# Layer 0: the recurrence's steps on VectorE and GpSimd regrouped, the global context moved into the couplings, the last output projection in two halves

## The reference, cut to what matters

```python
# attention: x + attn(demodulated x), 16 heads of 64
x = x + L0_attn(L0_cond(x, cond), W_qkv, W_out)
# gated recurrence over the 128 tokens, elementwise in the features
f = exp(-(W_f x + b_f));  i = exp(-(W_i x + b_i));  h = W_h x + b_h
#   (the kernel works with F = 1 + f, I = 1 + i, S = F + I + 1e-8 F I,
#    normalised gates I/S and F/S, and three scans along the tokens)
s = recurrence(initial = cond, gates, h)
# feed-forward: three cycles of couplings between features and their "twist"
g  = sigmoid(gc3(gelu(gc2(gelu(gc1(mean over tokens of s))))))   # global context
for cycle in range(3):
    c = base * sigmoid(cn4(gelu(cn3(gelu(cn2(gelu(cn1(s)))))))) + ... g
    s, twisted = s + c * twisted, twisted - c * s
x = x + s
```

## Time and profile before

| | |
|---|---|
| median of 3 runs | 1133.64 us |
| the profiled execution's own time | 1132.62 us |
| its span in the trace | 1131.3 us |
| PE busy | 1015.0 us, 90% of the span |
| DVE busy | 886.0 us, 78% |
| ACT busy | 770.5 us, 68% |
| POOL busy | 458.3 us, 41% |
| mean granted TensorE clock | 0.973 |
| attention of layer 0 with chunks 0 to 6 | start to about 482 us |
| couplings | about 487 to 575 us |

### The profile page before, as it was taken

How to read it: one execution, slowest core, us unless ns; L and a number is a source line. 1 busy time by engine, 2 the same in 40 slices (tenths; PEclk the granted TensorE clock), 3 DMA queues, 4 the chain that set the end, 5 groups by cost and what they waited for, 6 DMA issues and landing times.

```text
span 1131.3 us, 25531 instructions
## 1 busy us (share of the span) xinstructions
PE 1015.0 (90%) x8759; PEld 796.1 (70%) x8759; DVE 886.0 (78%) x3789; ACT 770.5 (68%) x2089; POOL 458.3 (41%) x531
## 2 busy tenths in 40 slices
PE   6999999999999999699889999997888888888677
PEld 5897878788878787533269888885766666665456
DVE  5676869686969686679988888886788888877796
ACT  5876667666766666468768778873677777776442
POOL 2434434343535353408700000006678877784001
PEclk9999999999999999899999999997999999999897
DMA  8000000000000000000000000000000000000002
GB/s 368 1 2 2 2 2 2 1 1 2 2 1 2 2 1 2 1 1 0 1 1 1 1 1 1 10 10 16 16 20 12 21 21 21 20 2 1 1 1 75
DMA packets 8577, 18.32 MB, mean 16 GB/s; under 512 B 1280, under 2 KB 5504, under 8 KB 8064
## 3 DMA queue, kind: packets, MB, share of 16 engines
q1 hardware_dynamic: 8448, 16.69, 4.3%
HBM read 10.39 MB, written 2.10 MB: 11 GB/s over the span
## 4 chain that ended last, share of the span: by engine, by line
PE 55%; DVE 20%; POOL 12%; ACT 8%; issue 5%; DMA 0%; DVEq 0%; ACTq 0%; SPq 0%; POOLq 0%
PE PB L407 5%; PE PB L241 5%; PE PB L242 5%; PE PB L243 5%; POOL AR_s L1525 5%; PE PB L391 4%; PE PB L336 4%; PE PB L374 4%; ACT W L355 3%; PE PB L1059 3%; PE PB L1060 3%; PE PB L1061 2%; DVE W L346 2%; PE PB L425 2%; PE PB L1537 2%
## 5 line engine op out<-in xcount | busy, mean ns | idle before, releaser
L355 ACT ACTIVATE W<-W,small 128x128 f32<-128x128 f32 x512 | 198.6, 390 | 141.8 <-DVE small L346 88.9
L366 POOL TENSOR_TENSOR W<-W,small 128x512 f32<-128x512 f32 x128 | 133.5, 1043 | 269.1 <-DVE small L360 269.1
L241 PE MATMUL PB<-RR_s 128*128 128x256 f32 (+3 forms) x544 | 176.8, 325 | 6.2 <-DVE AR_s L398 2.7
L242 PE MATMUL PB<-RR_s 128*128 128x256 f32 (+3 forms) x544 | 167.2, 307 | 0.0
L243 PE MATMUL PB<-RR_s 128*128 128x256 f32 (+3 forms) x544 | 167.2, 307 | 0.0
L1525 POOL TENSOR_TENSOR AR_s<-AR_s,small 128x512 f32<-128x512 f32 x128 | 129.6, 1040 | 34.9 <-DVE small L1518 34.9
L1033 ACT ACTIVATE AR_s<-PB,W 128x512 f32<-128x512 f32 (+2 forms) x160 | 100.5, 629 | 33.2 <-PE PB L243 28.6
L1047 DVE TENSOR_TENSOR RR_s<-AR_s,RR_s 128x512 fp32r<-128x512 f32 (+2 forms) x160 | 98.9, 622 | 29.7 <-ACT RR_s L1038 26.1
L241 PEld LDWEIGHTS PB<-RR_s 128*128 128x128 f32 x544 | 103.7, 191 | 17.2 <-issue 4.7
L346 DVE CUSTOM_DVE_ANT_0 W<-PB,W 128x128 f32<-128x128 f32 x512 | 113.1, 285 | 2.2
L1518 DVE CUSTOM_DVE_ANT_0 AR_s<-PB,W 128x128 f32<-128x128 f32 x512 | 111.5, 286 | 3.2 <-PE PB L1509 3.0
(11 more groups left out here) (356 smaller groups left out, 2376.5 us busy)
## 6 DMA issues: line engine op xcount, KB each, us to landing
W<-in_w SPq DMA_DIRECT2D x1, 5841.0 KB, 25.0
XF<-in_xT SPq DMA_DIRECT2D x4, 512.0 KB, 9.0
AR_s<-AR_s SPq DMA_DIRECT2D x32, 64.0 KB, 2.1
out<-XT SPq DMA_DIRECT2D x8, 256.0 KB, 2.4
W<-in_w SPq DMA_DIRECT2D x1, 1088.0 KB, 5.1
W<-in_w SPq DMA_DIRECT2D x1, 1024.0 KB, 7.9
QS<-AR_s SPq DMA_DIRECT2D x12, 64.0 KB, 2.1
KR<-AR_s SPq DMA_DIRECT2D x12, 64.0 KB, 2.1
```

What stands on the lines that cost most here:

```text
L241: nc.tensor.matmul(out, lh, rh, start=True, stop=False)
L242: nc.tensor.matmul(out, ll, rh, start=False, stop=False)
L355: e = nc.scalar.activation(SS[r][:, hl], SS[r][:, hl], ACTF.Exp, bias=mx[r][:, h:h + 1], scale=-1.0, accum_out=rc[r][:, h:h + 1])
L366: nc.gpsimd.tensor_tensor(s3, s3, over(rc[r], 2, [128, 4, 128]), ALU.mult).then_inc(s_nrm, 1)
```

## The change

Three edits, all in layer 0.

1. The steps of chunks 0 to 6 are numbered anew. GpSimd's two additions come at step 3 (turn V+1 in place of V+2), and the four reciprocals at steps 4 to 7 (two each in turns V+2 and V+3). GpSimd's two gates come at step 7 (V+3 in place of V+4), VectorE's addition of 1e-8 and GpSimd's h*F at step 8 (V+4 in place of V+5), and the backward scan at step 10 (the same turn V+5, now the only work of the recurrence there on VectorE). What follows stays. For chunk 7 the order on VectorE is the same as it was.
2. The global context of batch elements 0 to 23 leaves turns 64 and 65 of the attention and goes into turns 1 to 3 of the couplings, on banks of `plan3`.
3. The last output projection, `y` number 31, is done in two halves: the first pair of matmuls waits only for the copy of turn 62 and stands at the end of turn 65, the other pair in turn 66. The other projections wait for their two copies one after the other.

```diff
--- before.py
+++ after.py
@@ -221,8 +221,6 @@
                 c, i = divmod(s - 22, 16)
                 if 0 <= c < 7 and i < 3:
                     passes("fih"[i], c, *((s_fe, c + 1), (s_ie, c + 1), (s_gd, c * NGD + HC))[i])
-                if U < s < U + 4:
-                    passes("ctx", s - U - 1, s_cxa, s - U)
             if 0 <= v - 2 < NV:
                 passes("o", v - 2, s_ot, v - 1)
         for i in range(3):
@@ -397,15 +395,16 @@
             dve.wait_ge(s_pv, v + 1)
             nc.vector.tensor_copy(cs(OT[v // 2 % 2], v % 2), bank("o", v)[:, :]).then_inc(s_ot, 1)
 
-        def pe_y(j):
+        def pe_y(j, parts=range(4)):
 
             pe.wait_ge(s_wv, 16)
             pe_drained("y", j)
-            pe.wait_ge(s_ot, 2 * j + 2)
-            for p in range(4):
+            for p in parts:
                 o = (4 * (j % 2) + p) * 128
+                pe.wait_ge(s_ot, 2 * j + p // 2 + 1)
                 mm = nc.tensor.matmul(bank("y", j)[:, 0:256], w("wout", 128, o, o + 128), cs(OT[j % 2], p, 256), start=p == 0, stop=p == 3)
-            mm.then_inc(s_ym, 1)
+            if 3 in parts:
+                mm.then_inc(s_ym, 1)
 
         def dve_y(j):
             c = j // 2
@@ -448,26 +447,26 @@
                 nc.vector.tensor_scalar(IG, IG, 1e22, 1.0, ALU.min, ALU.add).then_inc(s_gd, 1)
                 dve.wait_ge(s_gd, o + GB)
                 nc.vector.scalar_tensor_tensor(SM, FG, 1e-8, IG, ALU.mult, ALU.mult).then_inc(s_gd, 1)
-            if i == 4 and c == CH - 1:
+            if i == 3 and c == CH - 1:
                 dve.wait_ge(s_gd, o + GSUM)
                 nc.vector.tensor_tensor(SM, SM, FG, ALU.add).then_inc(s_gl, 1)
                 dve.wait_ge(s_gl, p + PF)
                 nc.vector.tensor_tensor(SM, SM, IG, ALU.add).then_inc(s_gl, 1)
-            if 5 <= i < 9:
-                bl = bls[i - 5]
+            if 4 <= i < 8:
+                bl = bls[i - 4]
                 dve.wait_ge(s_gl, p + PI)
                 nc.vector.reciprocal(SM[:, bl], SM[:, bl]).then_inc(s_gd, 1)
-            if i == 9 and c == CH - 1:
+            if i == 7 and c == CH - 1:
                 dve.wait_ge(s_gd, o + GR)
                 nc.vector.tensor_tensor(IG, IG, SM, ALU.mult).then_inc(s_gl, 1)
                 nc.vector.tensor_tensor(FG, FG, SM, ALU.mult).then_inc(s_gl, 1)
-            if i == 10:
+            if i == 8:
                 dve.wait_ge(s_gl, p + PIN)
                 nc.vector.tensor_scalar(IG, IG, 1e-8, None, ALU.add).then_inc(s_gd, 1)
                 if c == CH - 1:
                     dve.wait_ge(s_gl, p + PFN)
                     nc.vector.tensor_tensor(SM, cs(HF, c), FG, ALU.mult).then_inc(s_gl, 1)
-            if i == 11:
+            if i == 10:
                 dve.wait_ge(s_const, 4)
                 dve.wait_ge(s_gd, o + GTF)
                 dve.wait_ge(s_gl, p + PNI)
@@ -498,16 +497,16 @@
         def pool_gated(c, i):
 
             o, p = c * NGD, c * NGL
-            if i == 4:
+            if i == 3:
                 pool.wait_ge(s_gd, o + GSUM)
                 nc.gpsimd.tensor_tensor(SM, SM, FG, ALU.add).then_inc(s_gl, 1)
                 pool.wait_ge(s_gl, p + PF)
                 nc.gpsimd.tensor_tensor(SM, SM, IG, ALU.add).then_inc(s_gl, 1)
-            if i == 9:
+            if i == 7:
                 pool.wait_ge(s_gd, o + GR)
                 nc.gpsimd.tensor_tensor(IG, IG, SM, ALU.mult).then_inc(s_gl, 1)
                 nc.gpsimd.tensor_tensor(FG, FG, SM, ALU.mult).then_inc(s_gl, 1)
-            if i == 10:
+            if i == 8:
                 pool.wait_ge(s_gl, p + PFN)
                 nc.gpsimd.tensor_tensor(SM, cs(HF, c), FG, ALU.mult).then_inc(s_gl, 1)
             if i == 11:
@@ -581,15 +580,14 @@
                 if 0 <= v - 1 < NV:
                     pe_T(2 * v - 1)
                 if v >= 4 and v % 2 == 0:
-                    pe_y(v // 2 - 2)
+                    pe_y(v // 2 - 2, range(4) if v < NV + 2 else (2, 3))
                 for s in (2 * v, 2 * v + 1):
                     if gate_step(s):
                         pe_gated(*gate_step(s))
-                    if U < s < U + 4:
-                        pe_drained("ctx", s - U - 1)
-                        pe_context(0, 24, s - U - 1, bank("ctx", s - U - 1), 0)
                 if 0 <= v - 2 < NV:
                     pe_PV(v - 2)
+                if v == NV + 1:
+                    pe_y(NV // 2 - 1, (0, 1))
 
         def act_attend():
             act.wait_ge(s_const, 2)
@@ -617,8 +615,6 @@
                 for s in (2 * v, 2 * v + 1):
                     if gate_step(s):
                         act_gated(*gate_step(s))
-                    if U < s < U + 4:
-                        act_context(0, 24, s - U - 1, bank("ctx", s - U - 1), 0)
 
         def dve_attend():
             dve.wait_ge(s_wc, 16)
@@ -667,7 +663,6 @@
                     nc.vector.tensor_scalar(ar07, w("ar"), 0.7, None, ALU.mult).then_inc(s_set, 1)
                 if v >= 4 and v % 2 == 0:
                     dve_y(v // 2 - 2)
-            dve_context(0, 24, 0)
 
         def pool_attend():
             nc.gpsimd.memset(pads, 0.0).then_inc(s_const, 1)
@@ -749,6 +744,8 @@
 
         def plan3():
             for t in range(19):
+                if 1 <= t < 4:
+                    passes3(("ctx0", t - 1), s_cxa, t)
                 for p, y, st in turn_steps(t):
                     m = 4 * y + p
                     if p == 3:
@@ -1233,6 +1230,9 @@
             pe.wait_ge(s_max, 4 * U)
             pe.wait_ge(s_pt, U)
             for t in range(19):
+                if 1 <= t < 4:
+                    pe_drained3(("ctx0", t - 1))
+                    pe_context(0, 24, t - 1, bank3(("ctx0", t - 1)), 0)
                 for p, y, st in turn_steps(t):
                     if p == 3:
                         pe_adapt(t)
@@ -1268,6 +1268,8 @@
                 if t == 17:
                     act_part(0)
                     act_part(1)
+                if 1 <= t < 4:
+                    act_context(0, 24, t - 1, bank3(("ctx0", t - 1)), 0)
                 for p, y, st in turn_steps(t):
                     if p == 3:
                         act_adapt(t)
@@ -1298,6 +1300,8 @@
                     dve_part(1)
                 for i in gate7_steps(t):
                     dve_gated(7, i)
+                if t == 3:
+                    dve_context(0, 24, 0)
                 for p in range(4):
                     for a in AGG.get(t, ()):
                         if a[0] == p:
```

## The result

| | before | after |
|---|---|---|
| median | 1133.45 us (4 runs, 1131.79 to 1134.16) | 1106.73 us (4 runs, 1106.22 to 1107.56) |
| ratio | | 0.9767, 95% interval 0.975 to 0.9784 |
| profiled execution, its span | 1132.62, 1131.3 | 1107.56, 1106.3 |
| mean granted clock | 0.973 | 0.974 |

What follows compares the result with a forecast made beforehand. Bound: VectorE's reciprocals wait for GpSimd's additions, stalling TensorE each chunk. 13.4 + 2.1 + 3.9 + 8.1 + 0.5 - 1.0 = 27.0 us off 1132.62 gives 1105.6, plus 1.0 for the runs' median: 1106.6 us, range 1100 to 1118.

Steps and rivals of the forecast that it cites:

- Steps 3 to 7: Chunks 0 to 5, turn V+2: reciprocals no longer wait for GpSimd, TensorE gains 2.23 us a chunk, 13.4 us in all.
- 161.3 and 161.4 of the working: Chunk 1, turn V+2: predicted times at which S is ready and at which VectorE comes for it.
- The clock: Steady part: without the stalls two falls of TensorE's clock to 1.2 GHz go, 1.95 us each, 3.9 us.
- Steps 8 and 10: Turn V+5: loses L466's 0.35 us of issue, shortening the wait at V+6's transposes; 2.1 us in all.
- L466 in V+4: Addition of 1e-8 beside GpSimd's work: 0.41 to 2.2 us, taken as 1 us, no net cost; at worst 2 us lost.
- Chunk 6 and the end: End of the attention: shorter stall, earlier copy, no wait for the last `y`; L415 8.1 us earlier.
- Into the couplings: From L415 to the first coupling: of the table load and context taken out, only 0.5 us arrive.
- The step on L805: Chunk 7: with the table load ahead of L432 gone, L805 starts 9.4 us earlier.
- The projections at low clock: Three projections after the attention may run at 1.2 GHz, 1.7 to 2.7 us later; at even odds -1.0 us.
- The sum: All terms together: 27.0 us off the profiled execution's 1132.62, so 1105.6; runs' median 1106.6 us.
- The "more" rival: Stalls in V+2 and at V+6's transposes go too, clock stays up at the end: 31 us, 1102.6; chance 0.12.

Runs made afterwards that it cites:

- e4: The changed kernel with GpSimd's two additions back at step 4 (turn V+2): 1129.78 us, ratio 0.999.
- e5: The kernel before with only GpSimd's two additions moved from step 4 to step 3 (turn V+1): 1112.73 us, ratio 0.9826.
- e1: The kernel before with only the new step numbers of chunks 0 to 6: 1105.85 us, ratio 0.9766.
- e12: e8 without the context's move into the couplings: 1094.08 us, ratio 0.9659.
- e3: The kernel before with only the last output projection in halves: 1128.27 us, ratio 0.9971.
- e2: The kernel before with only the global context moved into the couplings: 1133.24 us, ratio 1.0006.
- e6: The changed kernel with VectorE's addition of 1e-8 back in turn V+5 for chunks 0 to 6: 1108.11 us, ratio 0.9799.
- e11: The new step numbers and the context's move, without the halved last projection, against the kernel before: 1109.87 us, ratio 0.979.
- e9: The changed kernel measured once more, unaltered, on one chip beside other variants: 1107.25 us, ratio 0.9762.
- e7: The changed kernel with F, I and their product ahead of the bias of h in V+1, chunks 0 to 6: 1099.33 us, ratio 0.9728.
- e8: e7 with two of the four forward scans L486 moved from turn V+6 to V+7: 1096.58 us, ratio 0.9691.

## Why the prediction was right, and where its reasons were not

The forecast was 1106.6 us, the result 1106.73. The mechanism was right: S in time, two stalls of TensorE gone in each chunk, a shorter end of the attention. That the number is met so closely is luck. Executions of one program differ by several microseconds here. Besides, I had 1105.6 for the profiled execution and added 1.0, by which the runs' median lay above it before; the profiled execution took 1107.56, 2.0 more, and the median lay 0.8 below it. The two errors cancel. The terms one by one:

- **Steps 3 to 7, 13.4 us.** The wait is gone, the two stalls too. S was ready 0.05 us ahead of VectorE, as narrow as the 161.3 and 161.4 of the working. e4 takes away the additions' place alone and loses all of it; e5 makes that change alone and has chunks of 55.2 against 57.48, 2.26 less where I had 2.23. Shown.
- **The clock, 3.9 us.** The changed kernel and the nine others with the additions early (e1, e5 to e12) have no stretch of 2 us under 0.97 between 20 and 440 us. From the `y` at 94.28 to the one at 423.41 the kernel is 19.4 us shorter than before, as 13.4 + 2.1 + 3.9 had it, but it is made up a little differently. A chunk without a fall is 2.7 us shorter, where I had 2.58, about 16 us for six, and the two falls make about 3.3 (1.6 each, from e3). I priced one at 1.95 by a chunk of 57.48, while e3 has 57.79 for the same chunk without it. And a fall is a matter of the execution. With the stalls in place the traces have two (before), one (e2, e4) and none (e3). So the forecast took one execution for the rule.
- **Steps 8 and 10, 2.1 us: right size, wrong reason.** From e5 to the changed kernel a chunk shrinks from 55.22 (mean of three) to 54.86, 0.36 as predicted. But I gave it to the issue time of L466 leaving V+5, and e6 puts it back at a price of 0.06 on average. Counted from L279, the copy L396 comes after 2.47 us in e6 and 2.21 in the changed kernel, the first row maximum behind it after 3.07 and 2.97: the changed kernel has small gaps in that place, and they swallow 0.25 of the 0.35 us. The rest, 0.30 between e5 and e6, came with the other steps. GpSimd's h*F leaving V+5 is a part: beside it the subtraction L281 (L279 after) took 0.63 us (at 182.65 before, and at 176.96 in e5), without it 0.42 (at 177.09 above, and 0.43 in e6). That is 0.2; what is left I can't assign to single instructions, and no run moves h*F alone.
- **L466 in V+4.** Predicted 1 us, between 0.41 and 2.2; measured 0.91 in each of chunks 0 to 5, in the place of a reciprocal of 0.94. In chunk 1 it started beside the scaling that ended at 170.90 and was over at 171.19, before L511 was, and L511 took 1.46 us in place of 1.28. VectorE came in between two GpSimd instructions that follow without a gap. The rule of the Trainium skill (SBUF — State Buffer, Who interferes with whom), that whoever comes second waits for the whole instruction, agrees with the 0.62 us up to the scaling's end. That VectorE would wait for two in a row was my addition to it, and the gain of 25 us that I took from it was too low.
- **Chunk 6 and the end, 8.1 us.** From the `y` that the chain shows last in the steady part to the addition of `y` 31 it took 40.81 us before (441.83 to 482.64) and 32.64 after (423.41 to 456.05): 8.17. The low-clock `y` of 3.48 us became 1.89, the copy came when TensorE's work allowed it, and the wait for the last `y` went. e1 has all but 0.5 of it (33.17 us from 422.49 to 455.66), so the halves that I counted on for most of the last 1.89 us matter little when the clock is up.
- **Into the couplings, +0.5.** L863's place came out nearly as predicted: 20.82 us behind L415 before and 20.44 after, 0.4 where I had 0.5, and the same in e2. The step on L805 didn't: with the table load gone I had it 9.4 us earlier, where L863 had 8.6. By the two starts and the 19.4 us of the steady part it came 8.4 earlier (27.8 - 19.4), because it waited 0.62 us for VectorE's L442 to drain the bank of h. I had looked at who ended the wait, ScalarE, and not at what was next behind it.
- **The projections at low clock, -1.0.** Not in the changed kernel's first trace (2.84 us), in e1 and e12, but in seven of the ten traces with the additions early (4.2 to 5.4 in e5 to e11), e9 of the same program among them. It costs 1.6 us there: from L414 to L860 e9 takes 22.02, the first trace 20.44. So even odds were too kind, and their price about right. One reason given for it was wrong: "it was low in this place before" holds for the `y` ahead of the projections, not for themselves.

```profile
483.12 2.84 PE L425 MATMUL PB<-XF,W 128*128 128x512 f32 x6 [0.52 <-DVE XF L415]
```

- **The sum.** By the two profiled executions it is 25.1 us, where I had 27.0: 27.9 up to the first coupling, less 0.98 at the kernel's start and 2.0 behind that coupling, neither of which the change explains. By the medians it is 26.7.
- **The "more" rival** named a real reserve, two stalls that the change leaves. It didn't come true, as the first has its cause in V+1 and the second is VectorE's work in V+6. e7 and e8 take them: 1.05 and 0.5 us a chunk.

## What to carry to other kernels

When a fast engine waits for a slow one at the same place in every period, look at how early the slow one could have begun, and move its instruction one slot ahead before regrouping anything else: one step number gave 19 of 27 us here. Check the margin too: S was ready only 0.05 us ahead of its user. A gain that passes through an engine with gaps of its own is worth less than the issue time removed; put the instruction back alone to see. A stall of one or two microseconds on TensorE is also priced by the clock behind it, in some executions only, so count it as an average and don't read differences under 0.4% from four runs.

## What the runs showed of the hardware

- Two executions of the changed kernel, 1102.86 and 1107.56 us, are 0.4 us apart at 1000 us and 4.8 at the end, with 0.90 and 0.93 against 0.80 and 0.85 of granted clock in the last two stretches of 50 us. In the slower one it stands at 0.50, the 1.2 GHz level, from 1024 to 1040 us.
- Behind stalls of about 0.46 and 1.45 to 1.73 us the clock fell in some of equal chunks and not in others: two, one and none in three traces paced alike. A fall cost about 1.6 us of a chunk.
- An ACT table load is 1.28 us in every row. Edit 2 takes one out of the path and gave 0.38 us from L415 to L863 in the changed kernel, 0.37 in e2: behind the load stood another wait, and chunk 7's list on VectorE.
- Four L474 scans took 1.36 us with GpSimd idle (at 177.44) and 2.01 us with a GpSimd scaling running for their first 0.78 us (at 446.01). Four scans L483 took 1.37 us alone (at 475.77 before), and the same four, L482 after, 1.86 us with a scaling running for their first 0.62 us (at 183.02). VectorE lost about four fifths of the time for which both ran.
